# Layer-2 attention in a transformer kernel: another order of the key products, key sums from the second product, denominators last

## The reference

```
def _L2_attn_ref(inputs, W_Q, W_K, W_V, W_fc, gamma, beta):   # H, DK, DV = 16, 64, 64
    Q = sigmoid(inputs @ W_Q), K = sigmoid(inputs @ W_K), V = inputs @ W_V   # each B, N, H, 64
    KV = einsum('bnhk,bnhv->bhkv', K, V)
    num = einsum('bnhk,bhkv->bnhv', Q, KV)
    den = einsum('bnhk,bhk->bnh', Q, K.sum(axis=1))[..., None] + 1e-08
    x = (num / den).reshape(B, N, H * 64) @ W_fc + inputs
    return (x - mean(x)) * rsqrt(var(x) + 1e-5) * gamma + beta
x = x + _L2_attn_ref(_layernorm(x), ...)
```

## Time and profile before

| | |
|---|---|
| runs, device time | 2914.95 us median (2908.03, 2914.95, 2923.42) |
| span of the profiled execution | 2904.8 us; the profile gives no other time of it |
| TensorE matmul busy, share of the span | 2229.6 us, 77% |
| VectorE busy | 1746.7 us, 60% |
| ScalarE busy | 1105.2 us, 38% |
| GpSimd busy | 852.2 us, 29% |
| mean granted TensorE clock | 0.854 |

### The profile page before, as it was taken

How to read it: one execution, slowest core, us unless ns; L and a number is a source line. 1 busy time by engine, 2 the same in 40 slices (tenths; PEclk the granted TensorE clock), 3 DMA queues, 4 the chain that set the end, 5 groups by cost and what they waited for, 6 DMA issues and landing times. The chain is left out here.

```text
span 2904.8 us, 46677 instructions
## 1 busy us (share of the span) xinstructions
PE 2229.6 (77%) x13745; PEld 1703.0 (59%) x13746; DVE 1746.7 (60%) x4315; ACT 1105.2 (38%) x2728; POOL 852.2 (29%) x773
## 2 busy tenths in 40 slices
PE   4978959767477652377799972575999989989999
PEld 3865549746365540266466651464788745547887
DVE  5557965573477348860365568832566678855555
ACT  1753317541045101144444422353333356663332
POOL 2544525446413651276100010475000123201000
PEclk9998959965597556598899986797999989999999
DMA  4120001255604578165322237355000233310000
GB/s 154 40 62 2 1 35 41 62 182 122 181 5 175 112 182 163 35 124 119 92 60 57 47 94 139 73 121 119 1 0 0 63 72 93 91 40 5 7 7 12
DMA packets 282919, 217.01 MB, mean 75 GB/s; under 512 B 103107, under 2 KB 254448, under 8 KB 279696
## 3 DMA queue, kind: packets, MB, share of 16 engines
q1 hardware_dynamic: 248592, 181.06, 23.1%
q0 software_dynamic: 34176, 34.09, 7.2%
HBM read 148.95 MB, written 65.17 MB: 74 GB/s over the span
## 5 line engine op out<-in xcount | busy, mean ns | idle before, releaser
L162 POOL TENSOR_TENSOR fields<-ln_t,power 128x4 f32<-128x4 f32 x96 | 98.1, 1047 | 374.2 <-DVE ln_t L155 374.1
L3366 DVE TENSOR_REDUCE s_mx<-s_sa 128x2 f32<-128x512 f32 x256 | 165.3, 684 | 41.8 <-PE s_sa L3516 40.6
L3446 ACT ACTIVATE s_e<-s_sc 128x512 f32<-128x512 f32 x256 | 149.2, 600 | 85.8 <-PE s_sc L3535 83.0
L3112 PE MATMUL s_z<-s_t,s_mix_h 128*128 128x256 f32 x768 | 171.3, 379 | 0.0
L2017 POOL DMA_INDIRECT acc_dram<-s_yo,s_to_i x96 | 152.5, 1588 | 48.2 <-issue 26.7
L2005 POOL DMA_INDIRECT s_xg<-rows_dram,s_from_i x96 | 94.5, 985 | 223.7 <-DVE s_to_i L2138 195.6
L3112 PEld LDWEIGHTS s_z<-s_t,s_mix_h 128*128 128x128 f32 x768 | 146.0, 190 | 20.5 <-issue 1.0
L2322 PE MATMUL s_hu<-s_xgt,s_w 128*128 128x128 f32 x768 | 122.9, 308 | 8.9 <-issue 7.1
L191 PE MATMUL s_tp<-ident,xn 128*128 128x128 f32 x192 | 39.8, 345 | 109.2 <-DVE xn L181 107.3
L573 DVE SCALAR_TENSOR_TENSOR s_hs<-s_ha,s_b,s_sg 128x128 f32<-128x128 f32 x312 | 87.8, 344 | 50.4 <-issue 29.5
L3162 PE MATMUL s_z<-xnt,s_wt_w 128*128 128x512 f32 x256 | 116.6, 610 | 1.5 <-ACT xnt L197 1.5
(11 more groups left out here) (549 smaller groups left out, 6042.6 us busy)
## 6 DMA issues: line engine op xcount, KB each, us to landing
s_w<-in_L_ffn_W_dram SPq DMA_DIRECT2D x96, 256.0 KB, 3.0
acc_dram<-s_zero SPq DMA_DIRECT2D x32, 512.0 KB, 5.4
s_share<-share_dram SPq DMA_DIRECT2D x32, 512.0 KB, 6.0
fields<-acc_dram SPq DMA_DIRECT2D x16, 512.0 KB, 7.5
table_dram<-s_table_rows SPq DMA_DIRECT2D x2, 3136.0 KB, 10.5
s_wg<-in_L_ffn_w_gate_dram SPq DMA_DIRECT2D x64, 96.0 KB, 2.1
s_wu<-in_L_ffn_w_up_dram SPq DMA_DIRECT2D x64, 96.0 KB, 2.2
s_wd<-in_L_ffn_w_down_dram SPq DMA_DIRECT2D x64, 96.0 KB, 2.2
```

The source lines that it names most:

```text
L162: pool.tensor_tensor(core.rstd[:, tiles], core.ln_t[:, 2, tiles], core.power[:, 0:CT], ALU.pow).then_inc(s.scale_ready.sem, 1)
L3112: last = pe.matmul(bank(n)[:, o, :], weights[:, f, o * P:(o + 1) * P], src[:, f, :], start=f == 0, stop=f == HALF - 1)
L3366: dve.tensor_reduce(mx[:, i, t, 2 * pairs:2 * pairs + 2], sa[:, n % 2, :, :], AX.X, ALU.max).then_inc(max_done.sem, 1)
L3446: act.activation(e[:, n % RING, :, :], sc[:, n % 2, :, :], ACT.Exp).then_inc(exp_done.sem, 1)
```

## The change

Keys times inputs are summed with the inputs' 128 features as output rows: the inputs are the stationary operand and 512 key columns the moving one, 4 products in place of 16, and the result needs no transpose before the second product. The key sums now come from the second product: the inputs are lifted by 0.125 (`xa`, a copy made by VectorE), `wvo` gets a 129th column of 1/(128 x 0.125), and since normalised inputs sum to zero over their features, that column gives the key sum; so that the lift does not reach the other 128 columns, W_V is multiplied with a centring matrix (identity less 1/128) where it was transposed. The denominators, which need the key sums, move to the end of TensorE's half, behind the next query projection and two groups of the next key projection; `invert` moves behind `normal` and `add` in VectorE's body. The core of the diff:

```
-            pool.memset(xa[:, :, :, D:D1], 1.0).then_inc(filled.sem, 1)
+            pool.memset(wvo[:, :, :, D:D1], 1.0 / (D * LIFT)).then_inc(filled.sem, 1)
...
# VectorE: normal, start, body
-                    last = dve.tensor_scalar(xa[:, u, j, 0:D], core.x[...], core.mean[...], core.rstd[...], ...)
+                    last = dve.tensor_scalar(core.xn[:, u, j, :], core.x[...], core.mean[...], core.rstd[...], ...)
                 last.then_inc(s.xn_ready.sem, 1)
+                dve.drain()
+                dve.tensor_scalar(xa[:, u, :, :], core.xn[:, u, :, :], LIFT, None, ALU.add).then_inc(xa_ready.sem, 1)
...
+            dve.tensor_scalar(centre[:, :], core.ident[:, :], 1.0 / P, None, ALU.subtract).then_inc(centred.sem, 1)
             normal(0, 0, False)
...
                 for i in range(2):
                     b = 2 * c + i
-                    invert(b)
                     if i == 0 and after:
                         normal(c + 1, 1 - u, before)
                     if before:
                         add(b - 2, i)
+                    invert(b)
                     divide(b, u, i)
# ScalarE: keep_turned is gone, keep_kx is two plain copies of 512 columns to kxt,
# keep_m copies the key sums (first) and the 128 columns of each pair; body:
-                    keep_k(c, i)
+                    keep_k(c, i, range(2, 4) if i else range(4))
...
                     keep_kx(b)
-                    keep_turned(b)
-                    for h in range(2):
-                        if more:
-                            keep_q(c + 1, 1 - u, before, range(4 * h, 4 * h + 4))
-                        keep_m(b, i, h)
+                    keep_m(b, i)
+                    if more:
+                        keep_q(c + 1, 1 - u, before)
+                    if i == 0:
+                        keep_k(c, 1, range(2))
# TensorE: kx_products, m_products, start, body
+                pe.wait_ge(xa_ready.sem, xa_ready.past(c))
...
+                for h in range(HALVES):
                     for t in range(NT):
+                        last = pe.matmul(kn[:, h, :], xa[:, u, i * NT + t, :], ks[:, t, h * CW:(h + 1) * CW],
+                                         start=t == 0, stop=t == NT - 1)
+                    last.then_inc(kx_done.sem, 1)
...
+                            last = pe.matmul(kn[rows_a, M_BANK[p], first:first + D1], kxt[:, p, rows_a], wvo[:, a, p, :],
+                                             start=True, stop=True)
...
-                    last = pe.transpose(kn[:, h, n * P:(n + 1) * P], wv[:, p * P:(p + 1) * P], core.ident[:, :])
+                    last = pe.matmul(kn[:, h, n * P:(n + 1) * P], wv[:, p * P:(p + 1) * P], centre[:, :], start=True, stop=True)
...
-                    k_groups(c, u, i)
+                    k_groups(c, u, i, range(2, 4) if i else range(4))
...
                     kx_products(c, u, i)
-                    turn_kx(b)
-                    denominators(c, u, i, more)
                     if before:
                         out_product(b - 2, i, 1)
-                    for h in range(2):
-                        if more:
-                            q_groups(c + 1, 1 - u, range(4 * h, 4 * h + 4))
-                        m_products(b, h)
+                    m_products(b)
+                    if more:
+                        q_groups(c + 1, 1 - u)
+                    if i == 0:
+                        k_groups(c, u, 1, range(2))
+                    denominators(c, u, i, more)
```

More of the change, by code:

```diff
@@ L2356, in l2_attn @@
     D1 = D + 1
-    FIRST = 6
+    LIFT = 0.125
+    M_BANK = (2, 2, 2, 3, 3, 3, 0, 0)
+    M_PARTS = (range(0, 6), range(6, 8))
     LANES = 32
@@ L2369, in l2_attn @@
         ks = s.sb("ks", [P, NT, PAIRS * P])
-        xa = s.sb("xa", [P, 2, CT, D1])
-        wvo = s.sb("wvo", [P, 2, PAIRS, P])
-        kxs = s.sb("kxs", [P, PAIRS, P])
+        xa = s.sb("xa", [P, 2, CT, D])
+        wvo = s.sb("wvo", [P, 2, PAIRS, D1])
+        centre = s.sb("centre", [P, P])
         kxt = s.sb("kxt", [P, PAIRS, P])
@@ L2391, in l2_attn @@
         filled = s.sig("filled")
+        centred = s.sig("centred")
+        xa_ready = s.sig("xa_ready")
         wv_turned = s.sig("wv_turned")
@@ L2398, in l2_attn @@
         kx_done = s.sig("kx_done", 1)
-        kxs_ready = s.sig("kxs_ready")
         kss_ready = s.sig("kss_ready")
-        kx_turned = s.sig("kx_turned")
         kxt_ready = s.sig("kxt_ready")
@@ L2453, in normal @@
                     t = c * CT + j
-                    last = dve.tensor_scalar(xa[:, u, j, 0:D], core.x[:, bass.ds(t, 1), :].rearrange("p a d -> p (a d)"),
+                    last = dve.tensor_scalar(core.xn[:, u, j, :], core.x[:, bass.ds(t, 1), :].rearrange("p a d -> p (a d)"),
                                              core.mean[:, bass.ds(t, 1)], core.rstd[:, bass.ds(t, 1)],
@@ L2527, in keep_q, with keep_k @@
                     act.activation(qt[:, u, p, :], pj[:, p % 2, :], ACT.Sigmoid).then_inc(act_kept.sem, 1)
-            def keep_k(c, i):
-                for n in range(NT * HALVES):
+            def keep_k(c, i, groups=range(NT * HALVES)):
+                for n in groups:
                     t, h = n // HALVES, n % HALVES
@@ L2535, in keep_kx, with keep_m @@
             def keep_kx(b):
-                for part, (first, banks, count) in enumerate(((0, slice(0, 2), 3), (FIRST, slice(2, 3), 2))):
-                    act.wait_ge(kx_done.sem, kx_done.past(2 * b + part))
-                    pairs = slice(first, first + 3 * 2 if part == 0 else PAIRS)
+                for h in range(HALVES):
+                    act.wait_ge(kx_done.sem, kx_done.past(2 * b + h))
+                    act.activation(kxt[:, h * GROUP:(h + 1) * GROUP, :],
+                                   kn[:, h, :].rearrange("p (n d) -> p n d", d=P), ACT.Copy).then_inc(kxt_ready.sem, 1)
+            def keep_m(b, i):
+                for part, (banks, count) in enumerate(((slice(2, 4), 3), (slice(0, 1), 2))):
+                    act.wait_ge(m_done.sem, m_done.past(2 * b + part))
+                    pairs = slice(M_PARTS[part].start, M_PARTS[part].stop)
                     src = kn[:, banks, 0:count * D1].rearrange("p a (n v) -> p a n v", v=D1)
-                    act.activation(kxs[:, pairs, :].rearrange("p (a n) d -> p a n d", n=count), src[:, :, :, 0:D],
-                                   ACT.Copy).then_inc(kxs_ready.sem, 1)
                     for a in range(2):
@@ L2546, in keep_kx @@
                     last.then_inc(kss_ready.sem, 1)
-            def keep_turned(b):
-                for h in range(2):
[L2550 to L2557, removed]
+                    act.activation(ms[:, i, pairs, :].rearrange("p (a n) d -> p a n d", n=count), src[:, :, :, 0:D],
+                                   ACT.Copy).then_inc(m_kept.sem, 1)
             ln_act(act, core, s, 0, 0)
@@ L2562, in _ @@
                 act.wait_ge(wv_turned.sem, wv_turned.past(h))
-                act.activation(kxs[:, h * GROUP:(h + 1) * GROUP, :],
+                act.activation(kxt[:, h * GROUP:(h + 1) * GROUP, :],
                                kn[:, h, :].rearrange("p (n d) -> p n d", d=P), ACT.Copy).then_inc(wvt_kept.sem, 1)
@@ L2567, in _ @@
                 act.wait_ge(wvo_done.sem, wvo_done.past(n))
-                act.activation(wvo[:, a, h * GROUP:(h + 1) * GROUP, :],
+                act.activation(wvo[:, a, h * GROUP:(h + 1) * GROUP, 0:D],
                                kn[:, (2 + n) % 4, :].rearrange("p (n d) -> p n d", d=P), ACT.Copy).then_inc(wvo_kept.sem, 1)
@@ L2593, in turn_x @@
                 for j in range(CT):
-                    last = pe.transpose(s.tp[:, 0, j * P:(j + 1) * P], xa[:, u, j, 0:D], core.ident[:, :])
+                    last = pe.transpose(s.tp[:, 0, j * P:(j + 1) * P], core.xn[:, u, j, :], core.ident[:, :])
                 last.then_inc(s.tp_ready.sem, 1)
@@ L2603, in q_groups, with k_groups @@
                               start=True, stop=True).then_inc(projected.sem, 1)
-            def k_groups(c, u, i):
-                for n in range(NT * HALVES):
+            def k_groups(c, u, i, groups=range(NT * HALVES)):
+                for n in groups:
                     t, h = n // HALVES, n % HALVES
@@ L2613, in kx_products @@
                 b = 2 * c + i
+                pe.wait_ge(xa_ready.sem, xa_ready.past(c))
                 pe.wait_ge(m_kept.sem, m_kept.past(2 * b - 1))
                 pe.wait_ge(act_kept.sem, act_kept.past(16 * c + 8 + 4 * i + 3))
-                for p in range(PAIRS):
+                for h in range(HALVES):
                     for t in range(NT):
[L2618 to L2630, removed]
+                        last = pe.matmul(kn[:, h, :], xa[:, u, i * NT + t, :], ks[:, t, h * CW:(h + 1) * CW],
+                                         start=t == 0, stop=t == NT - 1)
+                    last.then_inc(kx_done.sem, 1)
             def denominators(c, u, i, ln):
@@ L2642, in denominators, with m_products @@
```

(14 more changed lines are left out.)

## The result

The changed kernel takes 2956.04 us (median of 2951.03 to 2956.84), before 2919.02 in the same comparison: a ratio of 1.0138, interval 1.0119 to 1.0158, so slower. The profiled executions differ by more, 2954.6 against 2904.8 us of span, 49.8 us. One run of before, in the comparison with experiments 5 and 6, took 3624.77 us at a mean granted clock of 0.608 and enters no ratio.

The account below looks back on a forecast made before the run. TensorE bounds the stage before; after the change VectorE's chain through the DRAM broadcast does. +47.4 us between inversions, +1.9 and +0.8 make +50.1 us: 2954.9 us of span, with 10.15 us outside it 2965 us, range 2948 to 2988.

Parts of the forecast that it names:

- The chain: VectorE's loop through the DRAM broadcast in layer 2's attention: turns of 21.46 and 23.16 us, 44.6 us a chunk, becoming the bound.
- `normal`'s new copy: VectorE's lifted copy of 128 x 512 in `normal`: between 0.25 and 0.69 us, taken at 0.69, making `normal` 1.7 us.
- The first inversion: Start of the attention stage: first inversion +1.9 us later, plus +0.8 us for preparing the stationary operand.
- TensorE's pace: TensorE's chunk in the stage: 22.72 + 15.28 = 38.00 us before, 35.3 us after the change.
- TensorE's slack: TensorE's denominators ready before VectorE comes back: 4.7 us early in one half, 7.4 us in the other.
- the second rival: TensorE's new gaps drop its clock to half and make its path late too; 2981 or 3043 us; 10% for visible cost.
- The span: Whole profiled execution: 2904.8 us plus the sum of +50.1 us gives 2954.9 us.
- the sum: Whole kernel: +47.4 us between first and last inversion (327.2 against 279.85), +1.9 first inversion, +0.8 start: +50.1 us.
- what follows the last inversion: Stage's end, the same chain of DMA, division and two `add`s as before: 0 us change.
- The time: Whole kernel's measured time: span of 2954.9 us with 10.15 us outside it, 2965 us, range 2948 to 2988.

Follow-up runs that it names:

- experiment 5: Changed kernel with invert back ahead of normal and add, and denominators directly behind the second product, so only the products remain: 2940.47 us, ratio 1.0078.
- experiment 6: Changed kernel whose division multiplies by a constant tile and does not wait for the broadcast, which is still issued: 2885.39 us, ratio 0.9885.
- experiment 1: Kernel before with only VectorE's new order, invert moved behind normal and add: 2958.88 us against 2910.19, ratio 1.0170.
- experiment 4: Changed kernel with add cut in two, the part up to the y read ahead of normal and invert, the rest between invert and divide: 2895.30 us, ratio 0.9953.
- experiment 2: Changed kernel with VectorE's old order, invert back ahead of normal and add; products and late denominators stay: 2955.17 us, ratio 1.0164.
- experiment 3: Changed kernel with the denominators directly behind the second product, ahead of the query and key projections: 2956.64 us, ratio 1.0153.

## Why the prediction was right, and where it was off

*The chain.* Right. Predicted 21.46, 23.16 and 44.6 us a chunk, 327.2 between the first and the last inversion; measured 21.43, 23.08 and 44.5 in the chunk shown, and 326.3. Experiments 1 and 6 show its two halves: the order alone makes it, the wait alone unmakes it.

*`normal`'s new copy.* Taken at 0.69 us, measured 0.43 (0.35 to the next instruction); `normal` is 1.57 us and not 1.7: between the bounds, and nearer the lower.

*The first inversion.* Predicted 1.9 + 0.8 = 2.7 us later, measured 1424.22 - 1421.80 = 2.4. Its parts miss by more and cancel: the key products begin only 0.1 us later and not 0.8 (1415.64 against 1415.53), because the query projection before them was 0.5 us shorter in this execution (mean granted clock 0.80 there, 0.75 before); from there to the inversion it takes 8.58 us and not 8.15.

*TensorE's pace.* The prediction's half of 22.72 us begins at 1574.63, which is the issue of SP's store; TensorE's half begins 0.42 us earlier, at the key projection:

```profile
1574.21 3.80 PE L2610 MATMUL s_pj<-s_wk,xnt 128*128 128x512 f32 x8
```

```profile
1608.89 0.69 DVE L2461 TENSOR_SCALAR s_den<-s_tp 128x512 f32<-128x512 f32 x1 [6.85 <-PE s_tp L2640]
```

So a chunk of before is 38.4 us (1574.21 to 1612.63, and 1570.47 to 1608.89 between inversions) and not 38.0, and less the 2.7 us it is 35.7 and not 35.3; experiment 4 shows 35.9. The forecast of the chain does not hang on it.

*TensorE's slack.* Predicted 4.7 us in the second half, measured 2.8. The clock, which falls in the gaps and is back by 1468.50, makes 1.6 us of the difference (turning 0.91 for 0.43, key products 4.60 for 3.44); nearly all of the rest is the half begun too late. So the mechanism of the second rival came, and in every one of the six second halves with a gap, whose key products take 4.5 to 4.8 us; it cost the changed kernel nothing because it fell into the slack, as that rival had priced it. In experiment 2, where TensorE's path was the bound, the same fall cost 2.2 us in the chunk shown (1.75 in the output product, 0.42 in the turning).

*The span.* Predicted 2954.9 us, measured 2954.6. That it is so close is in part luck: the stretch between the inversions came out 0.9 us under the sum, the first inversion 0.3 us, and what follows the last inversion 0.9 us over the forecast of no change (1204.1 us to the end of the span against 1203.2).

*The time.* Predicted 2965, measured 2956, inside the range. The term that was mis-sized is what lies outside the span: I took 10.15 us, the distance from the median to the span. The changed kernel's profiled run took 2956.31 us with 2954.6 of span: 1.7 us; in the runs of before in the experiments' comparisons it is 1.7 to 1.8 as well. So the profiled execution of before took about 2906.5 us, 8.4 us under the median of its runs, and I added that distance to the changed kernel too. That is also why the spans differ by 49.8 us and the medians by 37.0: the rise of 50.1 us that the sum gives fits the two profiled executions, but it is more than the medians show, whose interval ends at 46 us. In the comparisons the runs of before that count lie from 2903.7 us (mean clock 0.855) to 2923.6 us (0.850); what varies between them is not settled.

*What I did not see.* That late denominators have a price of their own, hidden here behind the order's. No forecast of the changed kernel hung on it, but the natural repair, putting `invert` back, fails on it (experiment 2). Relaxing the wait of the output product to the `add` before the last was not tried: `y`'s two slots lie in one tile of 512 columns (2 x 2 x 128), which TensorE would then write while VectorE reads it; no run shows what that does.

## What to carry to other kernels

An engine that works in program order and waits for a round trip of its own, as VectorE does here, pays that round trip in full (9.3 us) unless something stands between request and use. So when instructions are reordered, list what used to lie in each such wait. Add up the loop through the other engine before crediting time saved on the one that is busy: here 2.7 us a chunk less on TensorE bought nothing, because the loop through VectorE and the DMA, hidden under TensorE's 38.4 us before, grew to 44.5 us. Cut a block by who waits for its parts: the first 1.1 us of `add` released TensorE, and for the other 4.5 us TensorE did not wait (experiment 4).

## What was not expected of the hardware

An idle of 5.08 us on TensorE cost 2.2 us more after it ended, at a clock of 0.50 for the next 3.5 us, in a loop of 44.8 us (experiment 2); an estimate of such a wait by its length alone was short by 2.2 of 7.3 us. Not every gap has this price: behind the 3.62 us of experiment 5 the granted clock is 1.00 and the output product takes 1.86 us (1552.07 to 1553.93), while in three other chunks of the same run a gap of 3.0 to 3.4 us is followed by slow products; what decides it stays open. The broadcast hardly changed its length: VectorE's wait for it was 9.2 us at the longest before and 9.1 to 9.9 us in the changed kernel, and the longest in any run is 10.6 us, once in experiment 3.
